# First token mixer of a two-layer model in fp32: q and k projected channel-major, their convolution in passes of ScalarE and VectorE, norms folded into beta, v and RMS

## The reference

```python
q, k, v = (causal_conv_silu(x @ w, conv) for w, conv in ((w_q, conv_q), (w_k, conv_k), (w_v, conv_v)))   # 4 taps
q, k = l2norm(q), l2norm(k)                  # x * rsqrt(sum(x*x) + 1e-6), per head
beta = 2 * sigmoid(x @ w_b)
g = -exp(A_log) * softplus(x @ w_a + dt_bias)
def step(S, inp):                            # 16 heads, S is 64 x 128 per head
    q_t, k_t, v_t, g_t, b_t = inp
    S = S * jnp.exp(g_t)[..., None, None]
    mem = jnp.einsum('bhk,bhkv->bhv', k_t, S)
    delta = (v_t - mem) * b_t[..., None]
    S = S + jnp.einsum('bhk,bhv->bhkv', k_t, delta)
    return (S, jnp.einsum('bhk,bhkv->bhv', q_t * scale, S))
o = rmsnorm(o) * norm_w * silu(x @ w_g)      # per head
x = layernorm(x + o @ w_out)
```

## Time and profile before

| | |
|---|---|
| median of 3 runs | 5653.5 us (5652.21 to 5655.03) |
| the profiled execution | 5651.81 us, span 5650.0 us |
| granted TensorE clock, mean of the span | 0.94 |
| TensorE / VectorE / ScalarE / GpSimd busy | 5032.1 / 3759.0 / 2718.4 / 2258.5 us |
| first mixer, first window copy to last output | 67.9 to 2901.4 us |

### The profile page before, as it was taken

How to read it: one execution, slowest core, us unless ns; L and a number is a source line. 1 busy time by engine, 2 the same in 40 slices (tenths; PEclk the granted TensorE clock), 3 DMA queues, 4 the chain that set the end, 5 groups by cost and what they waited for, 6 DMA issues and landing times. The chain is left out here.

```text
span 5650.0 us, 104115 instructions
## 1 busy us (share of the span) xinstructions
PE 5032.1 (89%) x36634; PEld 3494.1 (62%) x36634; DVE 3759.0 (67%) x8878; ACT 2718.4 (48%) x6447; POOL 2258.5 (40%) x1588
## 2 busy tenths in 40 slices
PE   5999999999899999999989989996468787998998
PEld 3776776767677677776766645653146575664665
DVE  5656656666565665666658848845699846875884
ACT  1444444444344444444438838843410014874882
POOL 2424334243342433424337716713422115753761
PEclk7999999999999999999989989997689957998998
DMA  3000000000000000000010000000000000000000
GB/s 113 5 7 7 4 7 6 6 7 4 9 4 7 7 4 7 5 6 7 4 33 1 0 28 1 0 2 5 0 8 1 0 1 29 0 23 5 0 0 15
DMA packets 170263, 53.53 MB, mean 9 GB/s; under 512 B 142224, under 2 KB 166160, under 8 KB 169232
## 3 DMA queue, kind: packets, MB, share of 16 engines
q1 hardware_dynamic: 168736, 49.54, 3.8%
q10 hardware_dynamic: 1392, 2.20, 0.1%
HBM read 41.21 MB, written 10.49 MB: 9 GB/s over the span
## 5 line engine op out<-in xcount | busy, mean ns | idle before, releaser
L342 PE MATMUL gd_ps<-gd_taps,gd_xwin 128*128 128x512 f32 x2048 | 905.6, 598 | 8.0 <-ACT gd_qT L529 8.0
L342 PEld LDWEIGHTS gd_ps<-gd_taps,gd_xwin 128*128 128x128 f32 x2048 | 382.1, 190 | 464.5 <-issue 445.0
L788 POOL TENSOR_TENSOR gd_o_rn<-gd_tmp,gd_mhalf 128x8 f32<-128x8 f32 x64 | 103.5, 1635 | 1129.9 <-DVE gd_tmp L707 1129.9
L1299 ACT ACTIVATE L_ffn_s<-L_ffn_s,L_ffn_nb,L_ffn_r 128x128 f32<-128x128 f32 x1024 | 419.4, 482 | 3.1
L552 ACT ACTIVATE gd_X<-gd_ps 128x512 f32<-128x512 f32 x384 | 201.7, 645 | 419.9 <-PE gd_ps L384 419.9
L684 DVE TENSOR_TENSOR gd_Z<-gd_ps,cst 128x256 f32<-128x256 f32 x384 | 163.1, 425 | 323.5 <-PE gd_ps L422 257.6
L1119 POOL TENSOR_TENSOR L_ffn_t<-L_ffn_t 128x512 f32<-128x512 f32 x128 | 190.3, 1487 | 393.5 <-DVE L_ffn_t L1340 393.5
L782 POOL TENSOR_TENSOR gd_gate<-gd_gate,gd_norm_w 128x2048 f32<-128x2048 f32 x32 | 145.1, 4533 | 483.2 <-ACT gd_gate L517 483.2
L517 ACT ACTIVATE gd_v<-gd_ps 128x512 f32<-128x512 f32 x128 | 76.4, 597 | 406.2 <-PE gd_ps L342 406.2
L384 PE MATMUL gd_ps<-cst,gd_gV 128*128 128x128 f32 x1536 | 199.6, 276 | 53.8 <-DMA gd_gV<-gd_inverses 32.7
L1338 DVE TENSOR_TENSOR L_ffn_t<-L_ffn_ps,L_ffn_sb_rope 128x512 f32<-128x512 f32 x256 | 176.9, 691 | 101.7 <-PE L_ffn_ps L1144 101.7
(11 more groups left out here) (377 smaller groups left out, 13320.5 us busy)
## 6 DMA issues: line engine op xcount, KB each, us to landing
L_ffn_sb_rope<-in_rope SPq DMA_DIRECT2D x4, 2048.0 KB, 8.2
gd_tap_row<-in_L_attn_conv_v SPq DMA_DIRECT2D x2, 2048.0 KB, 7.0
gd_blocks<-gd_nA SPq DMA_DIRECT2D x256, 16.0 KB, 1.7
gd_Z<-gd_blocks SPq DMA_DIRECT2D x32, 128.0 KB, 2.0
gd_inverses<-gd_Z SPq DMA_DIRECT2D x32, 128.0 KB, 1.7
gd_gV<-gd_inverses SPq DMA_DIRECT2D x256, 16.0 KB, 2.0
L_ffn_sb_wqkv<-in_L_ffn_wqkv SPq DMA_DIRECT2D x4, 768.0 KB, 8.7
gd_tap_row<-in_L_attn_conv_q SPq DMA_DIRECT2D x1, 2048.0 KB, 15.4
```

What stands on the lines that cost most here:

```text
L342: ins = pe.matmul(ps[4 + i % 2][:], xwin[:, t:t + P] if i < 8 else xwin[:, PAD:PAD + P], taps[:, t, 512 * SLICE[i]:512 * (SLICE[i] + 1)] i ...
L1299: ins = act.activation(s[b][:, i, k], s[b][:, i, k], ACT.Exp, scale=r[b][:, h:h + 1], bias=nb[b][:, i, k:k + 1])
```

## The change

It touches `gated_delta` and the tables that are made of the inputs on the host. q and k are no longer projected with the tokens on partitions. Two heads (a pair, 128 channels) at a time, the plain weights are the stationary operand and 259 columns of x the moving one (`produce`), for 256 tokens, that is two chunks, at once. In an even chunk the eight pairs of k are made for the two chunks that follow, in an odd one the eight of q. ScalarE scales the product by the first tap (`first_tap`), VectorE adds the three other taps in three dependent passes over PSUM (`conv`), ScalarE applies SiLU. So q and k are never turned, but k is, once, for the state update (`turn_k`, copied to k_tok). GpSimd squares (`square`), TensorE sums the squares of each head over the partitions, with two columns of ones and zeros as the moving operand (`square_sums`). q and k are not multiplied by their norms: 1/|k|^2 goes into beta, |k| into v (`scale_v`), and |q|^2 into the epsilon of the output's RMS (`rms`). norm_w is folded into w_out once. Taps are folded for v only.

The order is new too. Small decay operations of the next chunk (`decays_first`, `decays_second`) stand between the levels of the solve, the a/b scores are made two chunks ahead, slices of v and pieces of q and k stand among the next chunk's decay sums and score products, and the batches are one sequence with no restart; the loop body holds four chunks.

```diff
+        def chunks(eng, body):
+            for b in range(B):
+                with eng.Fori(0, NC // GROUP - 1) as q:
+                    for j in range(GROUP):
+                        body(b * NC + (GROUP * q + j), b, GROUP * q + j, j, b * (NC // 2) + (2 * q + (j + 1) // 2), True, True)
+                for j in range(GROUP):
+                    c = NC - GROUP + j
+                    n = b * NC + c
+                    body(n, b, c, j, (n + 1) // 2, n < LAST, n < LAST - 1)
...
+                def produce(turn, j, i, b, c):
+                    if i >= 2:
+                        w(conv_s.now(turn, i - 2))
+                    elif i == 0:
+                        w(ab_s.now(turn))
+                    elif not (isinstance(turn, int) and turn < 2):
+                        w(c_s.now(turn - 1))
+                    pe.matmul(ps[6 + i % 2][:, PROD], w_pair[:, PAIRS * (j % 2) + i], xflat[:, bass.ds(b * (PAD + T) + c * P, XWIN)],
+                              start=True, stop=True).then_inc(qk_mm.sem, 1)
...
+                def square_sums(turn):
+                    for i in range(PAIRS):
+                        if i % 2 == 0:
+                            w(sq_s.now(turn, i // 2))
+                        for c in range(2):
+                            at = SUMS.start + 2 * PAIRS * c + 2 * i
+                            ins = pe.matmul(ps[6][:, at:at + 2], qk_sq[:, i, P * c:P * (c + 1)], cst[:, C_HALVES:C_HALVES + 2], start=True, stop=True)
+                    ins.then_inc(ss_mm.sem, 1)
...
+                def first_tap(turn, j, i):
+                    w(qk_mm.now(turn, i))
+                    at = PAIRS * (j % 2) + i
+                    act.activation(produced(j, i), ps[6 + i % 2][:, P:P + WIDE], ACT.Copy, scale=w_tap[:, at, 0:1]).then_inc(tap0_s.sem, 1)
...
+                    w(inv_k_s.now(s))
+                    dve.scalar_tensor_tensor(n_beta[:], t2, -2.0, k_inv[:, j % 2], ALU.mult, ALU.mult)
+                    dve.scalar_tensor_tensor(beta[:, j % 2], t2, 2.0, k_inv[:, j % 2], ALU.mult, ALU.mult).then_inc(beta_s.sem, 1)
...
+                def conv(turn, j, i):
+                    at = PAIRS * (j % 2) + i
+                    if i == 0:
+                        cc.start(turn)
+                    w(tap0_s.now(turn, i))
+                    for t in range(1, TAPS):
+                        ins = dve.scalar_tensor_tensor(produced(j, i), ps[6 + i % 2][:, P + t:P + t + WIDE], w_tap[:, at, t:t + 1],
+                                                       produced(j, i), ALU.mult, ALU.add)
+                        if t < TAPS - 1:
+                            cc.link(ins)
+                    ins.then_inc(conv_s.sem, 1)
+                    if i == PAIRS - 1:
+                        cc.end()
...
+                def rms(n, j):
                     for gi in range(0, G, 2):
                         w(osq_s.now(n, gi + 1))
                         two = tmp[4][:, HG * gi:HG * (gi + 2)]
-                        dve.tensor_scalar(two, two, EPS, None, ALU.add).then_inc(oss_s.sem, 1)
...
+                def body(n, b, c, j, s, follows, more):
+                    if follows:
+                        square_sums(n + 1, j + 1, s)
+                    residues(n)
+                    level(n, 0)
+                    if follows:
+                        decays_first(n + 1)
+                    level(n, 1)
+                    if follows:
+                        decays_second(n + 1, j + 1, s)
+                    level(n, 2)
+                    updates(n, j)
+                    if more:
+                        scores(n + 2)
+                    rms(n, j)
+                    if more:
+                        conv(n + 2, j, 0)
+                    gated(n, 0)
+                    if more:
+                        conv(n + 2, j, 1)
+                    gated(n, 1)
+                    if more:
+                        conv(n + 2, j, 2)
+                        conv(n + 2, j, 3)
+                    if follows:
+                        key_scores(n + 1)
+                        if more:
+                            conv(n + 2, j, 4)
+                        negative_decays(n + 1)
+                        if more:
+                            conv(n + 2, j, 5)
+                            conv(n + 2, j, 6)
+                            conv(n + 2, j, 7)
+                        query_scores(n + 1)
+                        inverse(n + 1)
+                    tail(n, b, c)
...
+                def body(n, b, c, j, s, follows, more):
+                    w(nrm_s.now(s if j % 2 == 0 else s - 1))
+                    for gi in range(3):
+                        scale_v(n, j, gi)
+                    if follows:
+                        w(yt_mm.before(n))
+                        for q in range(3):
+                            square(n + 1, j + 1, q)
+                    scale_v(n, j, 3)
+                    if follows:
+                        square(n + 1, j + 1, 3)
+                    w(last_s.now(n))
+                    for gi in range(G):
+                        if gi % 2 == 0:
+                            w(tk_out.now(n, gi // 2))
+                        pool.tensor_tensor(k_dec(gi), k_dec(gi), heads(last, gi).unsqueeze(2).to_broadcast([P, HG, DK]), ALU.mult).then_inc(kd_s.sem, 1)
+                    if follows:
+                        if j % 2 == 1:
+                            k_norms(n + 1)
+                        w(g_s.now(n + 1)); w(z_mm.now(n))
+                        growth(n + 1, 0)
+                        if more:
+                            window(n + 2, j, *ahead_of(b, c, 2))
+                        for gi in range(1, G):
+                            growth(n + 1, gi)
+                    root(n)
+                    if follows:
+                        masked_decays(n + 1)
```

More of the change, by code:

```diff
@@ new lines, in q_products @@
+                def q_products(n, j):
+                    w(silu_s.now(n - j % 2 + 1))
+                    for g0 in range(0, G, 2):
+                        w(nA_s.now(n, g0 + 1))
+                        if not (isinstance(n, int) and n == 0):
+                            w(yT_s.now(n - 1, g0 + 1))
+                        for k in range(HG):
+                            for gi in (g0, g0 + 1):
+                                at = pair(HG * gi + k)
+                                ins = pe.matmul(bank(gi)[:, k], kT(j, half(gi), at), qT(j, half(gi), at), start=True, stop=True)
+                                if k == HG - 1:
+                                    ins.then_inc(kq_mm.sem, 1)
@@ L378, in decay_sums, with state_products @@
                     for gi in range(G):
[L379 removed]
+                        w(gV_s.now(n, gi)); w(S_s.before(n, gi))
                         pe.matmul(ps[gi][:], cst[:, C_LATER:C_LATER + P], heads(gV, gi), start=True, stop=True).then_inc(log_mm.sem, 1)
[L382 removed]
+                def state_products(n, j):
+                    for g0 in range(0, G, 2):
+                        w(PT_s.now(n, g0 + 1))
+                        for k in range(HG):
+                            for gi in (g0, g0 + 1):
+                                at = pair(HG * gi + k)
+                                ins = pe.matmul(bank(gi)[:, k], kT(j, half(gi), at), S[half(gi), at], start=True, stop=True)
+                                if k == HG - 1:
+                                    ins.then_inc(ks_mm.sem, 1)
@@ new lines, in query_products @@
+                def query_products(n, j):
+                    for g0 in range(0, G, 2):
+                        if g0 == 0:
+                            w(gate_out.now(n, 3)); w(S_s.before(n))
+                        else:
+                            w(c_s.now(n))
+                            w(out_s.before(n))
+                            if not (isinstance(n, int) and n == LAST):
+                                w(ss_s.now(n + 1))
+                        for k in range(HG):
+                            for gi in (g0, g0 + 1):
+                                at = pair(HG * gi + k)
+                                ins = pe.matmul(ps[4 + gi][:, P * k:P * (k + 1)], qT(j, half(gi), at), S[half(gi), at], start=True, stop=True)
+                                if k == HG - 1:
+                                    ins.then_inc(qs_mm.sem, 1)
@@ L462, in turn_y, with output @@
                         ins.then_inc(yt_mm.sem, 1)
-                def output(n, groups):
-                    for gi in groups:
+                def output(n, more):
+                    if more:
+                        w(conv_s.now(n + 2))
+                    for gi in range(G):
                         w(yT_s.now(n, gi))
@@ new lines, in _ @@
+                project_ab(0, 0)
+                for i in range(PAIRS):
+                    produce(0, 0, i, 0, 0)
+                w(conv_s.now(0))
+                square_sums(0)
+                w(ss_s.now(0))
+                project_ab(1, 1)
+                for i in range(4):
+                    project_v(0, 0, i)
```

(31 more changed lines are left out.)

616 lines of the change are left out of this document (329 added, 287 removed).

## The result

The changed kernel takes 5599.7 us (median of 4 runs, 5598.79 to 5600.75) against 5652.85 us (5651.32 to 5655.03) for the kernel before: a ratio of 0.9904, 95% interval 0.9889 to 0.9919. It is faster by 53 us, under one per cent, but clear of the spread of the runs. The forecast was 213 us faster, at 5440, and 5599.7 lies 50 us above the range. The profiled execution took 5599.27 us, its span is 5597.3.

What follows compares the result with a forecast made beforehand. TensorE's list bounds the kernel now; after the change, a chain through VectorE, inverse and DRAM. Steps of 81 instead of 87.35 us gain 218, the start costs 6, the tail gains 1: -213, 5440 us; range 5380 to 5550.

Steps and rivals of the forecast that it cites:

- What is shared: VectorE and GpSimd holding each other: gated products beside masks 1.2 us, inverse beside decays of k 2.4, together 3.6 per chunk.
- the bounds: Step 77 to 79 without holds and with a faster first tap; 84.6 with holds behind each mask, slower sums, n_ec held.
- The second rival: VectorE and GpSimd take turns instruction by instruction over gated products, masks and key scores: step 86, 5595 us; 17%.
- The way through DRAM: From the inverse's end out to DRAM and back to the solve's start: 7.1 us per chunk.
- The boundary between batches: Between the two batches, today costing 21 us extra, becomes a step like others; 21 of the 218 us gain.
- The inverse: VectorE's 30 dependent steps before the solve: 7.2 us, plus 2.4 for holds by GpSimd's four decays of k.
- my own chain: Dependent work from the last state product to the next solve: +44.6 us, or +48.2 with 3.6 of holds.
- The first: Rival for the whole chunk: everything is hidden and TensorE's list is the bound; step 77, 5315 us; 8%.
- The third: Rival before the solve: TensorE's wait grows over 5 us and its clock falls; step 94, 5840 us, slower; 4%.
- The fourth: Rival: gain eaten entirely, step 87 to 88 and boundary lost to a longer start, within 0.2%; 2%.
- a wait before the solve would be released by the DMA: Sign: TensorE idle 2 to 3 us before the first turn of T, released by DMA.
- the first inverse step is released by the query scores: Sign: VectorE's first inverse step released by the query scores' end, not by the DMA; no size given.

Runs made afterwards that it cites:

- Experiment 1: Changed kernel with GpSimd's masks of the next chunk's decays made to wait for the gated products: 5449.88 us, ratio 0.9654 to the kernel before.
- experiment 8: Changed kernel with each of GpSimd's four masks of 512 columns made as four of 128: 5569.41 us, ratio 0.9855 to the kernel before.
- experiment 4: Changed kernel with masks behind the gated products, inverse ahead of the query scores, and sums of squares in fours behind the gate slices: 5381.61 us.
- experiment 7: Changed kernel with masks behind gated products, inverse before query scores, sums among gate slices, and eight chunks per group instead of four: 5344.84 us.
- experiment 6: Changed kernel with masks behind the gated products and sums in fours behind the gate slices, inverse still behind the query scores: 5494.17 us.
- experiment 2: Changed kernel with VectorE's inverse ahead of the masked query scores, masks left as they are: 5573.46 us, ratio 0.9864 to the kernel before.

## Why the prediction was wrong, step by step

**The step that failed** is the first of "What is shared": "One hold of a mask, 1.2 us; none at best; at worst one behind each of the four masks, 5 us. [...] I take 1.2 + 2.4 = 3.6." The gated products were held behind each of the four masks and by two scalings of v as well: 6.36 + 3.23 less 2 x 2.18, that is 5.2 us where 1.2 stood. Experiment 1 puts both behind the products, and the step falls from 86.18 to 80.69. The mechanism was seen, and its worst case was in the bounds; the count was wrong. I counted one hold because L630 was held once; but L630 is one instruction, and a row of products is held once for each instruction that the other engine has ready. What a single held instruction shows is the price of one turn. The number of turns was the smaller of the two engines' counts, four with four masks and eight with sixteen (experiment 8). The evidence for taking them all stood in the prediction: its masks run from +6.7 for 5.9 us, its gated halves from +6.4 to +8.6 and from +10.0 to +12.1.

The second rival named this mechanism and priced it: step 86, 5595 us. Measured: 86.18 and 5599.7. It got 17%, and no sum stands behind its 86, so that the figure fits so closely is partly luck: the bounds, with a hold behind each mask, came to 84.6 and 5550, the edge of the range. L630's one free run of 1.21 beside GpSimd's products does not speak against it, since that run had only to find GpSimd between two of them.

The Trainium skill, "SBUF — State Buffer", section "Who interferes with whom", says that the second to issue waits for the whole of the other's instruction, and that a GpSimd instruction which only writes does not contend. The trace agrees with both: 1.36 us beside a mask of 1.32, and 0.34 beside the memset of 1.80.

**How far that step goes.** In the chunk shown the solve starts at +52.85 instead of +48.2. The holds of the gated products beyond the one counted are 4.0 us of these 4.65; the terms below add some 1.8 and take 1.1 back, in the inverse. Over 31 steps 4.0 us are some 125 of the 160 us between forecast and result. The rest took the time past the range: the mean step, 86.18, lies 1.6 over the 84.6 of the worst case. The way through DRAM is 0.8 of that, the four jumps some 0.4, longer convolutions part of what is left.

**What followed from it.** TensorE's three waits for convolutions (4.72 us against my 2) come of the same hold, since the convolutions stand behind the gated products in VectorE's order. Behind them a slice of v ran at the lower clock (5.29 for 3.60), which the bounds did not have; with the waits gone (experiment 1) it takes 3.60.

**Terms that held.** The solve runs 32.52 us (32.6 predicted). The 32 sums of squares take 3.63 (3.6). The boundary between batches is a step like others. Without the masks' hold the key scores end at +19.54 (19.1) and the query scores at +31.02 (30.2). Once nothing else is in the way TensorE reaches the solve at +45.2 (experiment 4; predicted +45.7).

**Terms that were off.** A convolution pass takes 0.48 us (0.43). The small n_ec between convolutions takes 0.75 us beside a scaling of v, where its like takes 0.17. The inverse takes 8.5 us (9.6 with 2.4 of holds): all four decays of k hold a step of it, as predicted, but a held step takes 0.55 us where its like takes 0.22, so the four cost 1.3. The way through DRAM takes 7.9 us in this chunk (7.1). Products behind the block of sums run slow, 41 us in all by experiment 4. The jumps back were not in the sum; the steps over them were 12.7 us longer than without, and 28.9 once the rest was gone. The mixer's first product comes at 50.71, earlier than I had, but the first solve 84.8 us behind it (76): four more convolutions 9 us instead of 6, the scores 12 instead of 10, and 23.3 from the key scores' end to the solve, where I had put the 21 of the kernel before although my own chain made it longer. TensorE's wait of 3.09 us for the norms of q is not on that way: it waits another 2.35 for the DMA behind it.

**The other rivals.** The first, TensorE's list alone (77, 5315), is where experiment 7 comes to, at 78.03 and 5345, but only with four edits. The third did not happen in the changed kernel but before its last solve (a wait of 4.73 us, then 3.67 for the turn of T); experiment 6 shows it, and from waits of 2.2 to 3.5 us rather than the 5.23 that I gave. The fourth, no gain, did not come: the change is clear of the spread. That a wait before the solve would be released by the DMA was right (0.76 us in this chunk, none to 3.16 in the others up to the last; 2 to 3 predicted), and that the first inverse step is released by the query scores was too, but experiment 2 shows that this order costs 26 us, not the bulk.

## What to carry over

Where two engines can hold each other, put the two queues side by side over the stretch and count how many instructions of the one meet one of the other. A turn then lasts as long as the other's instruction: 1.28 us from start to start beside masks of 1.32, where the products otherwise follow each other at 0.26. So a hold costs about one us here, and it is paid as often as they meet. Then ask whether the holder is needed so soon: the masks start 5.9 us later in experiment 1 (+12.67 instead of +6.81) and nobody waits for them, and one wait in GpSimd's queue gave 150 us.

A list that becomes shorter on the engine that waits makes its wait longer, and a longer wait may cost more than itself. Experiments 4 and 6 hold the same edit, and it gains 41 us or loses 29 to 44 by whether the chain beneath was shortened first. The gain is well clear of the spread, the loss just so.

## What the runs showed that I had not expected

- Turns are strict: VectorE and GpSimd alternate one by one, at 1.28 us a turn with masks of 512 columns and 0.46 us with masks of 128.
- Behind 32 products with two columns out in a row (3.63 us) the granted clock is lower in 24 of the changed kernel's 31 chunks that have them: the next 64 products take up to 3.79 + 2.62 us (experiment 1) instead of 2.06 + 1.95. With the sums in fours behind products of 512 columns that is so in 3 of 31 (experiment 4).
- A jump back cost up to 5 us a time in the changed kernel and 2 to 13 in experiment 4, with packets on the queues of instructions crowding there. Inside the mixer the kernel before has no such packets.
- Before the first turn of T, a wait of 3.16 us left the clock up in the changed kernel and one of 3.01 in experiment 1; in experiment 6 it fell behind one of 2.17 and stayed up behind one of 2.63. The length of the wait does not decide it alone.
